# Attention on one core: the value products of two blocks of exponentials run behind each other, every second block

## The chip, the cores and the metric

The kernel runs on 1 core of one Trainium2 chip. The metric is the time of one execution on the device, in microseconds (us); lower is better. TensorE (PE in the rows, with its weight loads as PEld), VectorE (DVE), ScalarE (ACT), GpSimd (POOL) and SyncE (SP) each work through their own list of instructions in order, and wait for one another by semaphores.

## The reference

Two transformer layers of attention and feed-forward over x of 2 x 1024 x 256, in float32. The change touches the two attentions alone. Of these (cut; layer a has one key and value head shared by 16 query heads, layer b has 16 of each and a bias by distance):

```
qkv = x @ w_qkv + b_qkv
scores = jnp.einsum('bnhd,bmd->bhnm', q, k) / jnp.sqrt(jnp.float32(D))
scores = jnp.where(causal, -jnp.inf, scores)
attn = jax.nn.softmax(scores, axis=-1)
out = jnp.einsum('bhnm,bmd->bnhd', attn, v)
...
x = x + attn_a(layernorm(x)); x = x + ffn(layernorm(x))
x = x + attn_b(layernorm(x)); x = x + ffn(layernorm(x))
```

H = D = 16, 1024 positions, two batch rows.

## The kernel before, in words

Each attention (`attention(l)`, l = 0 and 1) is 8 steps: one step is one batch row and a group of 4 heads. A step computes the scores twice.

**Score units** (`query_major`, L1034): queries on the partitions, one PSUM bank of scores each. VectorE takes the row maximum of each (L1716; L1714 where the diagonal tile is masked in the same pass) and counts `su_used`. 38 units and a small transposition of the maxima make a step. They go to three banks in turn (`SU_BANKS`: bank 3, which is half of the tensor `st_ps`, and the two `su_ps`), so unit n waits until VectorE has finished unit n - 3. The maxima of step s+1 are made while step s runs; by L1745, L1721 to L1727 and three small DMAs (L640) they become extra rows of the queries for that step.

**Pieces** (`key_major`, L1075): keys on the partitions, 512 columns for one head each. ScalarE writes their exponentials into `pt` (L1437). Pieces also have three banks in turn, and piece n waits until ScalarE has finished piece n - 3. Four pieces (4 heads) make a **block**; step 0 of a layer has 10 blocks, the others 9, so that an attention has 73 blocks. `pt` is a ring of four blocks, and GpSimd zeroes the part of diagonal tiles behind the diagonal (L798).

**Values** (`values`, L1092): for one block, float32 matmuls with 32 columns of weights each, four side by side, accumulated in `o_ps`. In the trace, a matmul of this kind is two instructions, so that a block with 4 of them shows as x8, and one with two tiles of keys as x16. When the last block of an output half is in, ScalarE copies that half out (`take_output`, L1428); from the copied sums come inverses (SP's L645, VectorE's L1751, SP's L650 and L656), and GpSimd multiplies.

All is in an order written out by hand. In `attention(l)` of TensorE, after each piece come the units that `UNITS_BEHIND` has for it (about one a piece), and behind piece 1 of block i the values of block i - 2 (`PV_LAG = 2`). Twice per attention two blocks' values already run behind each other (at pieces 12 and 40, ahead of a piece), and once at the end.

## Time and profile before

| | |
|---|---|
| median of 3 runs | 1037.01 us (1034.52 to 1038.93) |
| the profiled execution | 1033.92 us, of which the span of its instructions is 1032.2 us |
| granted TensorE clock, mean | 0.984 of full |
| PE / DVE / ACT / POOL busy | 94% / 73% / 56% / 40% of the span |
| attentions | 55.65 to 299.8 us, and 574.14 to 806.8 us in the trace |
| one step (steps 3 to 5 of the first attention) | 27.94 us |

Busy shares are shares of the whole span. A busy PE is one that has a matmul under way; since matmuls overlap at their ends, a 100% share doesn't tell that it could do no more.

### The profile page before, as it was taken

The page shows a single profiled execution, that of the slowest core. Times are in us where ns is not written, and L with a number is a line of the kernel's source. Part 1 is how long each engine was busy: PE and PEld are TensorE (multiplying, and loading weights), DVE is VectorE, ACT ScalarE, POOL GpSimd, SP SyncE. Part 2 cuts the span into 40 slices and gives each one's busy share as a digit, 9 for nine tenths or more (in the row PEclk, how much of TensorE's full clock was granted, in tenths as well). Part 3 has the DMA queues.
Part 4 walks back from the last instruction along what each step waited for, and adds up shares of the span by engine and source line. Part 5 has one row for each costly group of instructions (what it writes and reads, how often), then busy time and mean ns, then how long its engine had stood idle before and what let it go on. Part 6 is the DMA issues. An engine that isn't in the chain of part 4 may idle for free.

```text
span 1032.2 us, 19370 instructions
## 1 busy us (share of the span) xinstructions
PE 969.5 (94%) x6562; PEld 625.6 (61%) x6562; DVE 750.2 (73%) x1820; ACT 573.1 (56%) x1078; POOL 409.4 (40%) x434
## 2 busy tenths in 40 slices
PE   4888999999889999999999899999999899999997
PEld 3433333333348889988886433443334588899887
DVE  6788888888346686447868988888882668754475
ACT  4525767777753335653445657777777533466432
POOL 3420635322534507716653202323225361374570
PEclk9969999999999999999999999999999999999999
DMA  4720222110205315644239524333401251266351
GB/s 142 189 50 10 66 44 45 42 41 13 48 9 172 125 46 156 187 114 129 82 93 217 137 41 71 64 64 77 75 14 44 84 174 51 82 192 158 118 183 48
DMA packets 66754, 95.40 MB, mean 92 GB/s; under 512 B 19669, under 2 KB 50821, under 8 KB 64599
## 3 DMA queue, kind: packets, MB, share of 16 engines
q1 hardware_dynamic: 46645, 52.74, 18.9%
q10 hardware_dynamic: 13100, 22.53, 8.7%
q0 software_dynamic: 6912, 18.88, 7.2%
q8 instruction: 55, 0.90, 0.4%
q14 instruction: 42, 0.34, 0.1%
HBM read 66.79 MB, written 26.67 MB: 91 GB/s over the span
## 4 chain that ended last, share of the span: by engine, by line
PE 72%; DVE 13%; DMA 4%; issue 3%; ACT 3%; POOL 2%; SPq 1%; ACTq 0%; DVEq 0%; POOLq 0%
PE o_ps L1092 13%; PE st_ps L1075 10%; PE su_ps L1034 8%; PE st_ps L284 7%; PE st_ps L285 6%; PE st_ps L286 6%; PE st_ps L1034 4%; PE o_ps L1232 3%; PE su_ps L1138 3%; PE su_ps L1232 3%; DVE mab L1716 2%; PE st_ps L1267 2%; DVE unread L1714 2%; DVE xn L1595 1%; PE su_ps L284 1%
## 5 line engine op out<-in xcount | busy, mean ns | idle before, releaser
L1437 ACT ACTIVATE pt<-st_ps 128x512 f32<-128x512 f32 (+1 forms) x584 | 314.7, 596 | 159.5 <-PE st_ps L1075 150.8
L1075 PE MATMUL st_ps<-qs,ks 99*128 99x512 bf16 (+9 forms) x768 | 212.5, 329 | 5.4 <-DMA qs<-nmx 3.3
L798 POOL TENSOR_SCALAR_AFFINE_SELECT pt<-pt 128x512 f32<-128x512 f32 x120 | 74.4, 637 | 315.3 <-ACT pt L1437 315.3
L1034 PE MATMUL su_ps<-ks,qs 102*128 102x512 bf16 (+7 forms) x538 | 160.0, 330 | 7.5 <-DVE mc L1716 2.8
L1092 PE MATMUL o_ps<-pt,vp 128*32 128x512 f32 (+3 forms) x1536 | 155.5, 502 | 0.0
L1716 DVE TENSOR_REDUCE mab<-su_ps 128x1 f32<-128x512 f32 (+2 forms) x211 | 137.6, 684 | 13.0 <-PE su_ps L1034 12.2
L1034 PEld LDWEIGHTS su_ps<-ks,qs 96*128 96x128 bf16 (+1 forms) x538 | 51.7, 98 | 109.2 <-DVE mab L1716 45.5
L879 POOL DMA_INDIRECT rows_in<-rows,source x80 | 78.6, 983 | 98.0 <-DVE source L1975 73.7
L1075 PEld LDWEIGHTS st_ps<-qs,ks 99*128 99x128 bf16 (+2 forms) x768 | 73.4, 99 | 65.3 <-ACT pt L1437 16.9
L1714 DVE CUSTOM_DVE_ANT_0 unread<-su_ps,cst 128x384 f32<-128x384 f32 (+1 forms) x168 | 99.4, 612 | 17.8 <-PE su_ps L1034 17.7
L1463 ACT CAST hh<-hf 128x512 fp32r<-128x512 f32 x64 | 39.7, 621 | 123.9 <-DVE hf L1930 121.7
L284 PE MATMUL st_ps<-xt_h,wu 128*128 128x512 f32 x256 | 100.9, 394 | 1.4 <-DVE source_f L1972 0.9
L285 PE MATMUL st_ps<-xt_h,wu 128*128 128x512 f32 x256 | 100.3, 392 | 0.0
L286 PE MATMUL st_ps<-xt_l,wu 128*128 128x512 f32 x256 | 99.7, 390 | 0.0
L889 POOL DMA_INDIRECT back<-outs,pos x64 | 67.6, 1056 | 61.8 <-DMA outs<-rows_out 41.6
L1034 PE MATMUL st_ps<-ks,qs 96*128 96x512 bf16 (+6 forms) x230 | 79.1, 357 | 5.5 <-DVE mc L1716 2.8
L1934 DVE TENSOR_TENSOR hl<-hf,hh 128x512 fp32r<-128x512 f32 x64 | 44.4, 694 | 42.6 <-ACT hh L1463 42.6
L1092 PEld LDWEIGHTS o_ps<-pt,vp 128*32 128x32 f32 x1536 | 35.7, 109 | 63.2 <-issue 38.9
L1716 DVE TENSOR_REDUCE mab<-st_ps 128x1 f32<-128x512 f32 (+2 forms) x99 | 67.7, 684 | 4.8 <-PE st_ps L1034 4.7
L1930 DVE TENSOR_TENSOR hf<-st_ps,sg 128x512 f32<-128x512 f32 x64 | 43.9, 686 | 28.1 <-PE st_ps L286 22.7
L1456 ACT ACTIVATE sg<-st_ps 128x512 f32<-128x512 f32 x64 | 38.2, 597 | 42.1 <-PE st_ps L286 41.9
L2035 DVE TENSOR_TENSOR rx_l<-st_ps,rx_h 128x512 fp32r<-128x512 f32 x40 | 27.6, 691 | 45.2 <-ACT rx_h L1487 45.2
(234 smaller groups left out, 2061.3 us busy)
## 6 DMA issues: line engine op xcount, KB each, us to landing
wu_raw<-w_units_dram SPq DMA_DIRECT2D x32, 384.0 KB, 3.2
outs<-rows_out ACTq DMA_DIRECT2D x40, 256.0 KB, 3.2
q_parts<-hml SPq DMA_DIRECT2D x16, 384.0 KB, 3.3
wexp_raw<-w_units_dram SPq DMA_DIRECT2D x16, 384.0 KB, 6.7
inv<-inverses SPq DMA_DIRECT2D x128, 32.0 KB, 1.8
rows<-xn SPq DMA_DIRECT2D x8, 512.0 KB, 6.0
qs<-q_parts ACTq DMA_DIRECT2D x10, 384.0 KB
k_parts<-hml SPq DMA_DIRECT2D x8, 384.0 KB, 2.9
```

Of the source, the lines that this page charges most:

```text
L284: pe.matmul(out, lh, rh, start=n == 0, stop=False)
L285: pe.matmul(out, ll, rh, start=False, stop=False)
L286: last = pe.matmul(out, lh, rl, start=False, stop=n == len(terms) - 1)
L798: pool.affine_select(block, block, [[0, 4], [1, P]], ALU.is_ge, 0.0, base=0, channel_multiplier=-1).then_inc(masked, 1)
L879: pool.indirect_dma_start(rows_in[:, n % RPAIRS, a, :], None, rows, bass.IndirectOffsetOnAxis(ap=source[:, 2 * i + a:2 * i + a + 1], axis= ...
L889: pool.indirect_dma_start(back[:, n % GBUFS, :], None, outs, bass.IndirectOffsetOnAxis(ap=pos[:, j, t:t + 1], axis=0)).then_inc(back_in[n ...
L1034: last = pe.matmul(out_b[:, c0:c0 + width], query_columns(s, slice(0, rows), j0 + a, P * qt, P * qt + P), key_stack(l, s)(j0 + a)[0:rows, ...
L1075: last = pe.matmul(out_b[:, at:at + hi - lo], key_stack(l, s)(j)[0:rows, P * kt:P * kt + P], query_columns(s, slice(0, rows), j, lo, hi), ...
L1092: last = pe.matmul(o_ps[32 * j:32 * j + 32, lo:hi], vp[:, QT * b + kt, 4 * g + j if l else 4 * (g % 2), :], exponentials(S, q)[:, j, at:at ...
L1437: act.activation(exponentials(S, q)[:, j, 0:width_of(s, q)], bank[KM_BANKS[i % len(KM_BANKS)]][:, 0:width_of(s, q)], ACT.Exp, scale=1 / np ...
L1714: dve.tensor_tensor_reduce(unread[ADDED.index(u) % 2][:, 0:width], src, later_keys[:, CH - width:CH], 1.0, LEAST, ALU.add, ALU.max, to).th ...
L1716: dve.tensor_reduce(to, src.rearrange("p (j k) -> p j k", j=share), AX.X, ALU.max).then_inc(su_used, 1)
```

## The change

Values no longer run one block at a time. `RUNS` says behind which block's piece 1 which blocks' values run, `EARLY_RUNS` ahead of which block's first piece, `LAST_RUN` what is left for the end. From block 10 on, the values of blocks i and i+1 run behind piece 1 of block i+3. The older of the two then waits a block longer, so that all four places of the ring are in use. In step 0 the runs are blocks 3 and 4, 5 and 6, and then 7, 8 and 9 ahead of step 1. The end has three blocks in place of two. An attention has 36 runs in place of 70 (each over the same 73 blocks). `take_output` moves with the run that completes the half, and the first reciprocal of a step moves from ahead of unit 6 to ahead of unit 9.

```
+def value_runs():
+    first = len(FIRST_BLOCKS)
+    runs = {2: (0,), 6: (3, 4), 8: (5, 6)}
+    early = {HALF_BLOCKS: (1, 2), first: (7, 8, 9)}
+    for i in range(first, block_base(STEPS) - PV_LAG - 1, 2):
+        runs[i + 1 + PV_LAG] = (i, i + 1)
+    done = max(b for run in runs.values() for b in run) + 1
+    return runs, early, range(done, block_base(STEPS))
...
+def taking(b):
+    i = run_behind(b)
+    if i is None:
+        i = next((i for i, run in EARLY_RUNS.items() if b in run), None)
+    return None if i is None else 4 * i + 3
...
-INVERT_AT, DIVIDE_BEHIND = (6, 27), (2, 4)
+INVERT_AT, DIVIDE_BEHIND = (9, 27), (2, 4)
...
-                    if n in (HALF_PIECES, FIRST_PIECES):
-                        for early in range(i - PV_LAG, i):
-                            values(l, 0, early)
+                    if j == 0:
+                        for b in EARLY_RUNS.get(i, ()):
+                            values(l, *place_of_block(b))
                     key_major(l, s, q, j)
-                    if j == PV_BEHIND and i >= PV_LAG and i not in [*range(HALF_BLOCKS, HALF_BLOCKS + PV_LAG),
-                                                                    *range(len(FIRST_BLOCKS), len(FIRST_BLOCKS) + PV_LAG)]:
-                        values(l, *place_of_block(i - PV_LAG))
+                    if j == PV_BEHIND:
+                        for b in RUNS.get(i, ()):
+                            values(l, *place_of_block(b))
...
-                for q in range(len(LATER_BLOCKS) - PV_LAG, len(LATER_BLOCKS)):
-                    values(l, STEPS - 1, q)
+                for b in LAST_RUN:
+                    values(l, *place_of_block(b))
...
-                        if s and n == 4 * PV_LAG - 1:
+                        own = piece_base(s) + n
+                        if s and own == taking(block_base(s - 1) + last_of(s - 1, 1)[0]):
                             take_output(S - 1, 1)
-                        if n == 4 * (last_of(s, 0)[0] + PV_LAG + 1) - 1:
+                        if own == taking(block_base(s) + last_of(s, 0)[0]):
                             take_output(S, 0)
```

On TensorE, blocks 2 and 3 of step 3 of the first attention, before the change. L1034 and L1038 are score units, L1075 pieces, L1092 values. First behind block 2's piece 1, where the values of block 0 stand alone:

```order
L1034 MATMUL su_ps<-ks,qs 128x512
L1075 MATMUL st_ps<-qs,ks 128x384
L1075 MATMUL st_ps<-qs,ks 128x128
L1092 MATMUL o_ps<-pt,vp 32x512 x4
L1034 MATMUL su_ps<-ks,qs 128x512
L1075 MATMUL st_ps<-qs,ks 128x384
```

and then behind block 3's piece 1, where the values of block 1 stand alone:

```order
L1034 MATMUL st_ps<-ks,qs 128x512
L1075 MATMUL st_ps<-qs,ks 128x512
L1092 MATMUL o_ps<-pt,vp 32x512 x4
L1034 MATMUL su_ps<-ks,qs 128x512
L1075 MATMUL st_ps<-qs,ks 128x512
```

In the changed kernel (its line numbers are 30 higher) the same stretch has nothing between unit and piece at the first place, and both blocks at the second:

```order
L1105 MATMUL st_ps<-qs,ks 128x128
L1064 MATMUL su_ps<-ks,qs 128x512
L1105 MATMUL st_ps<-qs,ks 128x384
...
L1064 MATMUL st_ps<-ks,qs 128x512
L1105 MATMUL st_ps<-qs,ks 128x512
L1122 MATMUL o_ps<-pt,vp 32x512 x8
L1064 MATMUL su_ps<-ks,qs 128x512
L1105 MATMUL st_ps<-qs,ks 128x512
```

The values of block 0 moved behind four more pieces and five more units, and stand ahead of those of block 1 with nothing between.

On ScalarE, from the middle of step 3 of the first attention into step 4: L1437 (later L1467) are exponentials, L1415 (L1445) issues of loads, L1428 (L1458) the copies of a finished output half. Before:

```order
L1415 DMA qs<-q_parts 16x4096
L1437 ACTIVATE pt<-st_ps 128x512 x10
L1428 COPY ou<-o_ps 128x512
L1437 ACTIVATE pt<-st_ps 128x512 x10
L1415 DMA qs<-q_parts 48x4096
L1437 ACTIVATE pt<-st_ps 128x512 x6
L1428 COPY ou<-o_ps 128x512
```

and in the changed kernel, from the same load on:

```order
L1445 DMA qs<-q_parts 16x4096
L1467 ACTIVATE pt<-st_ps 128x512 x14
L1458 COPY ou<-o_ps 128x512
L1467 ACTIVATE pt<-st_ps 128x512 x6
L1445 DMA qs<-q_parts 48x4096
L1467 ACTIVATE pt<-st_ps 128x512 x8
L1445 DMA qs<-q_parts 32x4096
L1467 ACTIVATE pt<-st_ps 128x512 x2
L1458 COPY ou<-o_ps 128x512
```

Both copies stand behind four more exponentials: that of step 3's first half (steps 1, 3, 5 and 7 have it so), and that of step 3's second half, which comes in step 4 (and likewise in steps 2 and 6).

## Rows read from the trace of the kernel before

**Rows 1.** Page, busy time of the engines in the whole span.

```profile
span 1032.2 us, 19370 instructions
PE 969.5 (94%) x6562; PEld 625.6 (61%) x6562; DVE 750.2 (73%) x1820; ACT 573.1 (56%) x1078; POOL 409.4 (40%) x434
```

**Rows 2.** Window of step 3: length, busy time (instructions), clock, DMA share, GB/s.

```profile
core 0: us, PE busy (x) PEld busy (x) DVE busy (x) ACT busy (x) POOL busy (x), PEclk, DMA share, GB/s
160.23:188.17 27.94, 27.52 (x210) 10.78 (x209) 24.59 (x62) 20.41 (x39) 10.77 (x11) 1.00 0.20 41
```

**Rows 3.** Timeline, TensorE around one run of values: start, length, engine, instruction.

```profile
170.41 0.38 PE L1075 MATMUL st_ps<-qs,ks 99*128 99x512 bf16 x1
170.72 1.06 PE L1092 MATMUL o_ps<-pt,vp 128*32 128x512 f32 x8
171.72 0.39 PE L1034 MATMUL su_ps<-ks,qs 96*128 96x512 bf16 x1
171.94 0.38 PE L1075 MATMUL st_ps<-qs,ks 99*128 99x512 bf16 x1
```

**Rows 4.** Timeline, TensorE, two blocks behind each other (512 and 256 columns), second attention.

```profile
612.05 1.50 PE L1092 MATMUL o_ps<-pt,vp 128*32 128x256 f32 x16
613.48 0.39 PE L1075 MATMUL st_ps<-qs,ks 105*128 105x512 bf16 x1
```

**Rows 5.** Timeline, VectorE around the run of rows 3; in brackets idle before.

```profile
171.24 0.68 DVE L1716 TENSOR_REDUCE mab<-st_ps 128x1 f32<-128x512 f32 x1
172.14 1.29 DVE L1716 TENSOR_REDUCE mab<-su_ps 128x1 f32<-128x512 f32 x2 [0.23 <-PE su_ps L1034]
```

**Rows 6.** Groups by shape in step 3: VectorE's score maxima, busy and idle before them.

```profile
L1716 DVE TENSOR_REDUCE mab<-su_ps 128x1 f32<-128x512 f32 x10 | 6.6, 686 | 1.3 <-PE su_ps L1034 1.3
L1714 DVE CUSTOM_DVE_ANT_0 unread<-su_ps,cst 128x384 f32<-128x384 f32 x6 | 3.3, 543 | 0.6 <-PE su_ps L1034 0.6
L1714 DVE CUSTOM_DVE_ANT_0 unread<-st_ps,cst 128x512 f32<-128x512 f32 x4 | 2.7, 687 | 0.2 <-PE st_ps L1034 0.2
L1714 DVE CUSTOM_DVE_ANT_0 unread<-su_ps,cst 128x512 f32<-128x512 f32 x4 | 2.7, 688 | 0.4 <-PE su_ps L1034 0.4
L1716 DVE TENSOR_REDUCE mc<-su_ps 128x4 f32<-128x512 f32 x1 | 0.7, 694 | 0.3 <-PE su_ps L1038 0.3
```

**Rows 7.** Waits in step 3, longest: engine, tile and line, what it waited for; us, times, longest.

```profile
PEld su_ps L1034 <- DVE mab L1716: 3.8, 5, 0.8
```

**Rows 8.** Timeline, VectorE around the two blocks of rows 4.

```profile
613.28 0.07 DVE L1714 DVE_READ_ACCUMULATOR2_ANT mc<- 128x1 f32 x1
614.13 0.69 DVE L1714 CUSTOM_DVE_ANT_0 unread<-st_ps,cst 128x512 f32<-128x512 f32 x1 [0.78 <-PE st_ps L1034]
```

**Rows 9.** Timeline, the same place of the first attention, TensorE and then VectorE.

```profile
101.92 2.53 PE L1092 MATMUL o_ps<-pt,vp 128*32 128x256 f32 x16
104.38 0.61 PE L1075 MATMUL st_ps<-qs,ks 99*128 99x512 bf16 x1
...
105.45 0.69 DVE L1714 CUSTOM_DVE_ANT_0 unread<-su_ps,cst 128x512 f32<-128x512 f32 x1 [2.23 <-PE su_ps L1034]
```

**Rows 10.** Windows ahead of and around the run of rows 9, and in step 7.

```profile
96.00:100.00 4.00, 2.18 (x20) 1.21 (x18) 3.48 (x12) 1.04 (x2) 0.00 (x0) 1.00 0.00 0
100.00:104.00 4.00, 3.41 (x20) 0.89 (x20) 3.21 (x12) 0.00 (x0) 0.00 (x0) 0.78 0.53 140
271.90:281.90 10.00, 9.49 (x58) 3.32 (x59) 0.25 (x1) 7.77 (x15) 4.67 (x6) 1.00 0.20 54
```

**Rows 11.** Timeline, ScalarE around the run of rows 3.

```profile
172.36 1.09 ACT L1437 ACTIVATE pt<-st_ps 128x512 f32<-128x512 f32 x2 [0.94 <-PE st_ps L1075]
```

**Rows 12.** Timeline, a finished output half: ScalarE's copy, then VectorE's reciprocal.

```profile
277.22 0.59 ACT L1428 COPY ou<-o_ps 128x512 f32<-128x512 f32 x1
279.74 0.25 DVE L1751 RECIPROCAL sums<-sums 128x16 f32<-128x16 f32 x1 [10.53 <-DMA sums<-ou]
```

**Rows 13.** Timeline, end of the first attention, TensorE.

```profile
297.76 2.09 PE L1092 MATMUL o_ps<-pt,vp 128*32 128x512 f32 x16
```

More of the change, by code:

```diff
@@ L161, in place_of_block, with run_behind @@
     return next((s, i - block_base(s)) for s in reversed(range(STEPS)) if i >= block_base(s))
+def value_runs():
[6 more added lines that the diff above has]
+    return runs, early, range(done, block_base(STEPS))
+PV_LAG = 2
+RUNS, EARLY_RUNS, LAST_RUN = value_runs()
+def run_behind(b):
+    return next((i for i, run in RUNS.items() if b in run), None)
+def taking(b):
[3 more added lines that the diff above has]
+    return None if i is None else 4 * i + 3
 def unit_base(S):
@@ L215 @@
 FC_BEHIND = {10 + 3 * t: t for t in range(QT)}
-PV_LAG = 2
 PV_BEHIND = 1
-INVERT_AT, DIVIDE_BEHIND = (6, 27), (2, 4)
+INVERT_AT, DIVIDE_BEHIND = (9, 27), (2, 4)
 QKV = [[("kv", 0), ("q", 0), ("q", 1)],
```

## The prediction

> **What bounds the kernel now.** I read the page first: TensorE is busy 94% of the span and VectorE 73% [rows 1], which invites the view that all that counts is TensorE's time. The shares mix attentions with feed-forward, so next came windows of one step: of 27.94 us TensorE is busy 27.52, VectorE 24.59, ScalarE 20.41 [rows 2]. A busy TensorE isn't yet one that can do no more, since a stalled matmul's neighbours overlap it. So third the waits inside that step: its weight loads for score units wait for VectorE, 3.8 us in 5 waits in the largest group alone [rows 7]. And VectorE waits too: the idle before its score maxima sums to 1.3 + 0.6 + 0.2 + 0.4 + 0.3 = 2.8 us, always for a score unit from TensorE [rows 6]. Fourth the timeline, to see when. It is always the same: while TensorE runs values, it issues no score units. VectorE works through what lies in the three banks and then stands. In the run at 170.72, VectorE is busy until 171.24 + 0.68 = 171.92, which is 1.20 after the run's start, and goes on at 172.14, which is 0.42 after the unit behind the run started at 171.72 [rows 3, 5]. So two engines run in lockstep with little slack either way: TensorE is ahead for a while and waits for a bank, then it is away for values and VectorE waits. Work on VectorE plus its idle time is the step's time, and that sum is what I forecast with.
>
> **What a merged run saves on TensorE.** A run of one block (512 columns) takes from 170.72 to the next unit at 171.72, 1.00 us. One of 512 and 256 columns takes from 612.05 to 613.48, 1.43 us [rows 3, 4]. 256 columns more cost 0.43, so 512 cost 0.86, and 0.14 is paid once per run. Before the run there are 0.31 from the piece's start to the run's, where 0.22 pass between a unit and a piece of the same width (171.72 to 171.94): 0.09 more, also once per run. A merge saves 0.14 + 0.09 = 0.23 us, and two blocks of 512 take 1.86. Each attention goes from 70 runs to 36: 34 merges, 68 in all, 68 x 0.23 = 15.6 us, if TensorE's time were all. The end of the first attention shows a dearer pair: 2.03 us, by the record of 2.09 less the 0.06 by which the record of rows 3 (1.06) is longer than that run [rows 3, 13]; there the second block waits for its last exponentials, so I take 1.86 and keep 2.0 as the bound at which nothing is saved.
>
> The Trainium skill (TensorEngine Tiling (Array Packing), Key Properties) says that a change of tiling mode drains the engine. The fixed 0.23 agrees in kind. By that rule alone the sum would be the 15.6 us gain; it stands as the first rival below.
>
> **What it costs VectorE.** How long the banks last after a run's start: mean idle at the nine runs of the step is 2.8 / 9 = 0.31, so VectorE has work for 1.00 + 0.42 - 0.31 = 1.11 us. With a run of 1.86, it stands 1.86 + 0.42 - 1.11 = 1.17 us. There are three banks as before: that cover can't double because the run does. 9 blocks are 4.5 runs a step: 4.5 x 1.17 = 5.3 against 2.8, so 2.5 more. Two things are to be taken off. The idle shown is smaller than the time lost: two maxima behind each other last 1.29 where one lasts 0.68 [rows 5], they overlap by 0.08, which each restart loses; 4.5 restarts fewer give back 0.36. And in every second step the run behind block 7 is gone, where VectorE makes the small parts of the maxima (0.3 idle at `mc` [rows 6]): 0.2 a step. Left: +1.9 us a step.
>
> Bounds: the longest cover I find is 1.30 (613.28 + 0.07 against the start at 612.05 [rows 4, 8]). With 1.25 everywhere, since TensorE has eight pieces in which to fill all banks, it is 4.5 x 1.03 = 4.6, and +1.3 a step; without the 0.2, and with runs of 1.9, +2.3. Does TensorE get that far ahead? Between two merged runs are 8 pieces and about 8.4 units at 0.22 each, 3.6 us; VectorE needs for 8.4 units of 0.60 about 5.0. Yes: it fills the banks, waits for VectorE, and the 0.23 that it saved becomes more waiting for banks.
>
> The mechanism isn't only arithmetic, the trace has it. At the 1.43 us run VectorE stands 0.78 [rows 8]; my formula gives 1.43 + 0.22 (a piece comes before the unit) + 0.42 - 1.30 = 0.77. At the same place in the first attention the run takes from 101.92 to 104.38, 2.46 us (the clock is at half there, 0.78 in the window), and VectorE stands 2.23 us [rows 9, 10].
>
> VectorE makes maxima in steps 1 to 6 but for the last two blocks of step 6, so 12 steps less 2 x 0.2, 11.6 for both attentions: 11.6 x 1.9 = 22 us.
>
> The Trainium skill (Perfetto Trace Analysis, Optimization Strategy) says that the same gap repeating can mean too little PSUM for the next tile. Rows 5 agree, and it speaks against this change, which leaves the three banks and lengthens the gap.
>
> **The rest of the edits.** Step 0: two merges in each attention, 0.4 each in the first and about nothing in the second, +1 (0 to 1.5, my choice by the gaps above). Ahead of step 1 stand three blocks, 0.85 longer than now, less one run's idle of about 0.4: +0.45, and +1 in the first attention where the clock is at half: +1.5. Step 7 has no score units: ScalarE and TensorE share it, ScalarE busy 7.77 and TensorE 9.49 of 10.0 us [rows 10]. ScalarE starves longer per merged run (it stands 0.94 at a run of 1.00 already in step 3 [rows 11]), TensorE saves 0.23 per merge where projections load it: nothing, -1.5 to +2. The end: now the last two blocks take 2.03; with a third ahead of them that once ran 1.5 us earlier, the pieces are issued earlier by as much; nothing, up to +0.5. The ring adds no wait: the place of block i+4 is freed by a run that TensorE issues before that block's first piece. The later copies: from copy to reciprocal pass 279.74 - 277.22 = 2.5 us [rows 12]; now 6 pieces lie between, 4.7 us at 27.94 / 36 a piece, and the reciprocal moved from unit 6 to 9 for it. Hidden by maxima; without that cover it would stop VectorE up to 2.5 us once a step.
>
> Sum: 22 + 1 + 1.5 = 24.5 us. The profiled execution has 1033.9, so 1058.4; it is 3.1 below the median of 1037.0, against which I forecast **1061 us**.
>
> **Rivals.**
> 1. TensorE's time decides, the saving arrives: 1037 - 15.6 = 1021. For it: 27.52 of 27.94 busy, and no TensorE wait of note outside weight loads. Against: VectorE's idle and work alone fill the step, and a longer absence must lengthen the idle unless cover grows to 1.86 + 0.42 - 2 x 0.31 = 1.66, more than any in the trace. From there on the gain begins. 0.11. Another 0.02 for a part of it (covers of 1.5).
> 2. A wash, within 0.5%: cover of about 1.4 to 1.5, so that idle per pair grows by less than 0.3. For it: in parts of the step TensorE isn't yet full ahead, and with eight pieces between runs it always is. 1032 to 1042. 0.08.
> 3. The forecast, VectorE starved at each run, 1051 to 1070. 0.74.
> 4. Beyond it something more: ScalarE starves as well and its lateness meets VectorE's in TensorE's order, or the clock falls to half as behind the stretch with TensorE 2.18 of 4.0 us busy [rows 10]. After the change a step has TensorE at some 25.5 of 29.8, far from that. Above 1070. 0.05.
>
> **How the numbers follow.** A measurement here tells about 0.5% from no change. Faster is 0.13, same 0.08, slower 0.79. The likeliest case's own range comes from the bounds: 11.6 x 1.3 - 0.5 = +14.5 gives 1051, 11.6 x 2.3 + 6 = +33 gives 1070. This holds 0.74; to leave out no more than 0.2 the range goes down over the wash: 1037 to 1070.
>
> **What would show it.** In the changed trace: runs of two blocks 1.86 us from start to the next unit; steps 1 to 6 of 29 to 30.5 us instead of 27.94, those with an even number, which have five runs, longer than those with four; VectorE's idle before score maxima 5 us a step in gaps of 1.0 to 1.3, all released by TensorE; more weight-load waits for VectorE; no reciprocal waiting for its sums. If instead the gaps are 0.6 or less, my cover is wrong, and the kernel is faster. If steps are longer but the gaps aren't at the runs, the cause is another.

## The result and the profile after

The changed kernel takes 1093.71 us (median of 4 runs, 1093.08 to 1095.71) against 1036.09 for the kernel before on the same chip: ratio 1.0555, 95% interval 1.0537 to 1.0572. That is 57.6 us slower. The direction was forecast, the size wasn't (1061 us), and the time lies outside the range.

From the page after, the line that answers to [rows 1], and two groups before which the idle time (behind the last bar) grew, from 5.4 and 17.8 us:

```profile
PE 998.1 (91%) x6562; PEld 632.6 (58%) x6562; DVE 750.8 (69%) x1820; ACT 570.2 (52%) x1078; POOL 409.6 (38%) x434
...
L1105 PE MATMUL st_ps<-qs,ks 99*128 99x512 bf16 (+9 forms) x768 | 217.3, 333 | 21.6 <-DMA qs<-nmx 13.9
...
L1745 DVE CUSTOM_DVE_ANT_0 unread<-su_ps,cst 128x384 f32<-128x384 f32 (+1 forms) x168 | 98.9, 610 | 45.9 <-PE su_ps L1064 45.8
```

No engine is busier in its share: TensorE's fell from 94% to 91%, VectorE's from 73% to 69%. The second row holds what no step of the forecast had: TensorE waits 13.9 us for transfers of the maxima (3.3 us before).

Windows after, of steps 2 and 3 of the first attention, the last 3.7 us of step 3, and the first 4 us of step 4 (columns as in [rows 2]):

```profile
137.55:170.01 32.46, 31.50 (x225) 11.68 (x226) 23.24 (x58) 19.66 (x37) 12.07 (x14) 0.93 0.15 35
170.01:203.53 33.52, 28.86 (x194) 10.81 (x193) 25.87 (x65) 20.86 (x40) 10.27 (x11) 0.95 0.17 34
...
199.80:203.53 3.73, 1.34 (x5) 0.32 (x6) 2.48 (x10) 1.90 (x4) 0.00 (x0) 1.00 0.05 9
203.53:207.53 4.00, 4.00 (x27) 1.26 (x27) 0.86 (x3) 1.20 (x2) 0.00 (x0) 0.57 0.41 91
```

A step takes 32.5 and 33.5 us where [rows 2] had 27.94; 29.8 was forecast. At the end of step 3 TensorE is busy for 1.34 of 3.73 us, and right behind it the granted clock is 0.57, mostly the lower level of 1.2 GHz. From the start of step 0 to that of step 7 the attentions take 27.2 and 28.5 us longer, 55.7 of the 59.6 us between the two spans (1032.2 and 1091.8); the rest lies between and behind the attentions.

A merged run after, TensorE and then VectorE (timeline; answers to [rows 3, 5]):

```profile
212.51 1.92 PE L1122 MATMUL o_ps<-pt,vp 128*32 128x512 f32 x16
214.36 0.39 PE L1064 MATMUL su_ps<-ks,qs 96*128 96x512 bf16 x1
...
213.03 0.68 DVE L1747 TENSOR_REDUCE mab<-su_ps 128x1 f32<-128x512 f32 x1
214.79 0.69 DVE L1747 TENSOR_REDUCE mab<-su_ps 128x1 f32<-128x512 f32 x1 [1.09 <-PE su_ps L1064]
```

The run takes 1.85 us to the next unit, and VectorE stands 1.09 us where it stood 0.23 [rows 5] (0.08 more in each, if the overlap of two maxima is counted as the forecast did: its 1.17). At this run the forecast's size is in the trace to the digit; over whole steps it is checked in e1 below, where the queue doesn't disturb it.

The end of step 3 after, in order of time: VectorE's last part of the maxima, ScalarE's copy of the finished first half, SyncE's two issues, TensorE's first piece of step 4:

```profile
195.14 0.28 DVE L1758 TENSOR_TENSOR nmx<-nmr,nmx 32x128 bf16<-32x128 f32 x1
...
199.15 0.58 ACT L1458 COPY ou<-o_ps 128x512 f32<-128x512 f32 x1
...
199.75 0.58 SPq L675 DMA_DIRECT2D sums<-ou  x1
200.38 1.82 SPq L670 DMA_DIRECT2D qs<-nmx  x3
...
203.53 0.56 PE L1105 MATMUL st_ps<-qs,ks 99*128 99x512 bf16 x1 [2.37 <-DMA qs<-nmx]
```

The maxima are ready at 195.42, but their transfers leave at 200.38. SyncE issues in order, and ahead of them stands the transfer of the first half's sums, which waits for the copy. The same place before:

```profile
182.46 0.59 ACT L1428 COPY ou<-o_ps 128x512 f32<-128x512 f32 x1
...
183.43 0.60 DVE L1727 TENSOR_TENSOR nmx<-nmr,nmx 32x128 bf16<-32x128 f32 x1
...
183.08 0.59 SPq L645 DMA_DIRECT2D sums<-ou  x1
184.06 1.83 SPq L640 DMA_DIRECT2D qs<-nmx  x3
```

There the copy came first, and the maxima left 0.03 us after their last part. Now the copy, which moved with its run, is the later of the two in odd steps.

### The profile page after: what moved, and what is told of

Its sections match the earlier page's. It is cut to its first block, busy times and chain, and to the rows that moved or that the text cites. A ratio compares the mean times of both kernels' runs of the same rounds, so it can differ in the third digit from the quotient of the medians.

```text
span 1091.8 us, 19370 instructions
## 1 busy us (share of the span) xinstructions
PE 998.1 (91%) x6562; PEld 632.6 (58%) x6562; DVE 750.8 (69%) x1820; ACT 570.2 (52%) x1078; POOL 409.6 (38%) x434
## 3 DMA queue, kind: packets, MB, share of 16 engines
q1 hardware_dynamic: 46645, 52.74, 17.8%
## 4 chain that ended last, share of the span: by engine, by line
PE 62%; DVE 17%; issue 7%; DMA 6%; ACT 3%; POOL 3%; SPq 2%; ACTq 0%; DVEq 0%; POOLq 0%
PE o_ps L1122 13%; PE st_ps L1105 6%; PE st_ps L314 6%; PE st_ps L315 6%; PE st_ps L316 6%; PE su_ps L1064 5%; DVE mab L1747 5%; PE o_ps L1262 3%; PE su_ps L1262 3%; PE su_ps L1168 3%; DVE unread L1745 3%; PE st_ps L1064 2%; POOL rows_in L909 2%; DMA qs<-nmx 2%; PE st_ps L1297 1%
## 5 line engine op out<-in xcount | busy, mean ns | idle before, releaser
L1467 ACT ACTIVATE pt<-st_ps 128x512 f32<-128x512 f32 (+1 forms) x584 | 311.4, 602 | 219.3 <-PE st_ps L1105 210.0
L1105 PE MATMUL st_ps<-qs,ks 99*128 99x512 bf16 (+9 forms) x768 | 217.3, 333 | 21.6 <-DMA qs<-nmx 13.9
L1064 PE MATMUL su_ps<-ks,qs 102*128 102x512 bf16 (+7 forms) x538 | 163.5, 335 | 11.4 <-DVE mab L1747 3.9
L1122 PEld LDWEIGHTS o_ps<-pt,vp 128*32 128x32 f32 x1536 | 45.7, 119 | 74.8 <-issue 58.6
L1745 DVE CUSTOM_DVE_ANT_0 unread<-st_ps,cst 128x512 f32<-128x512 f32 (+1 forms) x88 | 54.9, 624 | 16.8 <-PE st_ps L1064 16.8
```

The source lines that it names most:

```text
L1064: last = pe.matmul(out_b[:, c0:c0 + width], query_columns(s, slice(0, rows), j0 + a, P * qt, P * qt + P), key_stack(l, s)(j0 + a)[0:rows, ...
L1105: last = pe.matmul(out_b[:, at:at + hi - lo], key_stack(l, s)(j)[0:rows, P * kt:P * kt + P], query_columns(s, slice(0, rows), j, lo, hi), ...
L1122: last = pe.matmul(o_ps[32 * j:32 * j + 32, lo:hi], vp[:, QT * b + kt, 4 * g + j if l else 4 * (g % 2), :], exponentials(S, q)[:, j, at:at ...
L1467: act.activation(exponentials(S, q)[:, j, 0:width_of(s, q)], bank[KM_BANKS[i % len(KM_BANKS)]][:, 0:width_of(s, q)], ACT.Exp, scale=1 / np ...
L1745: dve.tensor_tensor_reduce(unread[ADDED.index(u) % 2][:, 0:width], src, later_keys[:, CH - width:CH], 1.0, LEAST, ALU.add, ALU.max, to).th ...
```

## The experiments

Ratios are to the kernel before in the same set of runs, with 95% intervals; it had 1036 to 1038 us in two sets and 1072 to 1075 in four (see the end), so step lengths are compared as well. Steps are read as pairs, odd and even, since merged runs fall four to the one and five to the other.

**The queue apart from the runs.** e1: the changed kernel, SyncE's order turned.

```
+                    if s == 0:
+                        gather_sums(S, 0)
-                    gather_sums(S, 0)
                     if s + 1 < STEPS:
                         send_maxima(l, s + 1)
+                    if s:
+                        gather_sums(S, 0)
```

> The changed kernel with one edit on SyncE: in steps 1 to 7 the three small transfers of the next step's maxima are issued ahead of the transfer of the first half's sums, and no longer behind it. Queue theory (the copy of the first half came four exponentials later in odd steps, SyncE waits for it ahead of the maxima, and so TensorE waits at the start of steps 2, 4 and 6, after which its clock falls): waits for the maxima's transfer at a step's start fall from 13.9 us to under 4, most of the half clock in the attentions goes, time 1058 to 1070. Bank theory alone (VectorE starved 1.17 us at each merged run, and nothing else matters): steps of about 29.8 us would already be all of it, the time stays near 1094. If the banks cost nothing and the queue all: 1021 to 1036.

Measured: 1.0246 (1.0231 to 1.0261), 26.6 us over before. Windows of e1, steps 2 and 3:

```profile
132.87:163.15 30.28, 29.33 (x226) 11.17 (x225) 24.43 (x64) 20.14 (x39) 12.06 (x14) 1.00 0.17 37
163.15:192.51 29.36, 27.07 (x194) 10.57 (x193) 24.64 (x60) 20.15 (x39) 10.25 (x11) 1.00 0.20 39
```

Mean 29.82, which is 1.88 over 27.94. (Over steps 2 to 5 of both attentions the mean is 30.07; one of these eight has a fall of the clock in it.) VectorE's idle before its score maxima is 9.6 us in these two steps, 4.8 a step, in nine gaps of 0.8 to 1.2, one for each merged run: the picture that the forecast named ahead. In steps 2 and 3 of the changed kernel it was 17.4 us, the longest gap 3.8. Less than half of the 57.6 us is left once the queue is turned.

e2: the kernel before with single runs, its copy four pieces later in odd steps, and the first reciprocal of a step three units later.

```
-INVERT_AT, DIVIDE_BEHIND = (6, 27), (2, 4)
+INVERT_AT, DIVIDE_BEHIND = (9, 27), (2, 4)
-                        if n == 4 * (last_of(s, 0)[0] + PV_LAG + 1) - 1:
+                        if n == 4 * (last_of(s, 0)[0] + PV_LAG + 1 + s % 2) - 1:
```

> The kernel before, its values one block at a time, with one piece of the change alone: in odd steps ScalarE's copy of the first half stands four exponentials later, and the first reciprocal ahead of unit 9 in place of 6. Queue theory: SyncE issues the maxima some 2.5 us later in steps 1, 3 and 5 of both attentions, the margin at the step's start was about 0.4, so about 2 us in 6 steps, 12 us, and with falls of the clock up to 22: 1046 to 1060. Bank theory: no change, 1036, idle of VectorE at a run still 0.31.

Measured: 1.0179 (1.0164 to 1.0195), 19.9 us over. No run is merged, and yet the longest group of TensorE's waits is this:

```profile
PE st_ps L1075 <- DMA qs<-nmx: 12.4, 8, 2.9
```

The late copy and the late reciprocal cost by themselves nearly as much as the merged runs. Not all of it is the wait for the maxima: step 1 of the second attention takes 33.42 us, where e1 and e3 have 28.64 and 28.19, and in it VectorE's reciprocal waits for its sums. SyncE and then VectorE there:

```profile
654.32 3.43 SPq L656 DMA_DIRECT2D inv<-inverses  x4
657.79 0.61 SPq L645 DMA_DIRECT2D sums<-ou  x1
...
661.92 0.25 DVE L1751 RECIPROCAL sums<-sums 128x16 f32<-128x16 f32 x1 [3.54 <-DMA sums<-ou]
```

The sums' copy had ended at 651.60; their transfer stood behind the inverses' in the same queue. The kernel before has no such wait at this place. e2 doesn't separate the reciprocal's shift from the copy's.

e3: values three blocks behind, runs single (`runs[i + 1 + PV_LAG] = (i,)` for all blocks), maxima sent first.

> The changed kernel with the maxima's transfers issued first, and with the values one block at a time again from block 10 on, but each three blocks behind (so all four ring places are used, and copies stand late, and nothing is merged). Bank theory: VectorE's idle per run is back at 0.3, steps back at about 28 us, time 1033 to 1041. If instead the older values or the full ring cost something, it stays over 1045.

Measured: 0.9995 (0.9975 to 1.0015), steps of 27.95. The ring, the lag, the late copies and the new order together cost nothing; pairing is what costs in e1.

**What the queue and the runs cost together.** e1 and e2 sum to 46.5 us of 57.6. In the trace after, the granted clock is at half for 3.4 or 6.8 us around the starts of steps 2, 4 and 6, where before it isn't. f1 puts work of TensorE into those waits, and z1 is the changed kernel beside it. (Cut: the wait for the piece's bank moves ahead of the filler, which writes to that bank.)

```
+                if j == 0 and q == 0 and s in (2, 4, 6):
+                    for _ in range(10):
+                        pe.matmul(out_b[:, 0:P], ident, ident, start=True, stop=True)
```

> The changed kernel, and ahead of the wait for the transfer of the maxima at the start of steps 2, 4 and 6 of each attention ten fp32 matmuls of the identity with itself (128 columns each, by the sizes of the others about 0.2 us each, so 2 us) into the bank that the piece overwrites. They stand in a wait of 2.4 to 3.9 us. Question: in the changed kernel TensorE's granted clock is at half for 3.4 or 6.8 us in eight more places than before the change, four of them in attention steps behind a start of a step that waits for the maxima. Theory A (the clock falls because TensorE stood still at those starts): the falls that begin behind the starts of steps 2, 4 and 6 go, those near other places stay, and the time is 5 to 12 us below that of the changed kernel without the filler, in spite of up to 1 us that the filler may add at each of six starts. Theory B (the falls come from the merged runs' bursts or from something else than the stand-still): the falls stay, and the time is 0 to 6 us above.

> The changed kernel itself, on the same chip as the three others of this set, so that they can be compared with it directly: its ratio to the kernel before was 1.056 on another chip. If the chip's own slower feed-forward part (1072 instead of 1036 us for the kernel before) adds the same to both kernels, its ratio here is (1072 + 57.6) / 1072 = 1.054; both theories on the cause (the bank of scores that comes free late plus the queue of transfers that the late copy holds up) expect that.

Measured: z1 1.0549 (1.0521 to 1.0577), f1 1.0399 (1.0375 to 1.0423). Work that computes nothing makes the kernel 13.1 us faster. Timeline of f1 at the start of step 4, then the windows of 4 us on either side:

```profile
198.10 2.40 PE L1102 MATMUL st_ps<-cst 128*128 128x128 f32 x20
200.65 0.39 PE L1108 MATMUL st_ps<-qs,ks 99*128 99x512 bf16 x1 [0.15 <-DMA qs<-nmx]
```

```profile
196.50:200.65 4.15, 3.95 (x28) 2.64 (x26) 2.88 (x11) 2.30 (x5) 0.00 (x0) 1.00 0.05 8
200.65:204.65 4.00, 4.00 (x33) 1.36 (x34) 1.82 (x6) 1.77 (x4) 0.00 (x0) 1.00 0.45 100
```

At this place the clock is 1.00 and not 0.57. The six falls at those starts are gone. At other places (ahead of step 1, inside step 3, in the feed-forward part) they are still there; against z1 one inside step 5 is gone, and two are new, at 290 and 785 us. Those inside odd steps start right behind TensorE's wait for the transposition of the maxima, in the changed kernel as well:

```profile
189.40:193.40 4.00, 2.50 (x15) 0.98 (x13) 3.79 (x11) 3.38 (x7) 0.84 (x2) 1.00 0.08 8
```

The clock falls at 193.4. In the kernel before no fall begins inside steps 1 to 6. An odd step of f1 takes 33.54 or 33.55 us with such a fall, and 31.91 or 32.01 without. Theory A holds, with slightly more than its 12 us. The Trainium skill (TensorE: Matmul & The Clock Gate, What's actually happening) says that a gate sets the clock by how busy TensorE has been of late; these two traces agree. The 13.1 us are of the size of the 11.1 that e1 and e2 leave over; that they are the same microseconds was not measured.

**Why pairing costs 1.9 us a step.** First VectorE is relieved: in h1 (single runs) and h2 (the runs and queue of e1) its maximum of a unit off the diagonal reads 64 of 512 columns, so 7/8 of those columns are left out.

```
+                    if s and not diagonal:
+                        src = src[:, 0:64]
```

> The kernel before, with VectorE's maximum from step 1 on taken over the first 64 of 512 columns of each unit that is not diagonal (16 units a step); the maxima of the other columns are left out, so the exponentials differ in value but not in number. VectorE's busy time in a step falls from 24.6 of 27.9 us by 16 times about 0.45 us = 7 us or more, and units no longer wait for it. Both theories expect TensorE (27.5 us of a step busy by the records) to set the time then: 5 to 20 us faster than before, the time of a step 26.8 to 27.7 us. It is here for the next kernel.

> The changed kernel with the same shortened maxima, and with SyncE sending the maxima ahead of the sums of the first half (as in the run that had the merged runs without the held-up queue). Theory A (the forecast's: a merge itself saves TensorE 0.23 us, and costs only because VectorE has two banks of scores to live on while a run of 1.86 us passes): with VectorE at 17 of 27.9 us it can stand idle in the run and catch up, so merging is a gain here: 8 to 16 us faster than the kernel with short maxima alone (68 merges by 0.23 us = 15.6 us). Theory B (a merged run itself costs TensorE time: by its clock, its reads or the wait for both exponentials): it stays slower than the kernel with short maxima alone by 5 us or more.

Measured: h1 0.9955 (0.9937 to 0.9973), the lower end of what was expected, h2 1.0107 (1.0072 to 1.0141). Windows of step 3 in h1, then of steps 3 and 4 in h2:

```profile
156.18:183.88 27.70, 27.35 (x211) 10.86 (x209) 17.98 (x62) 20.37 (x39) 10.77 (x11) 1.00 0.19 42
```

```profile
159.02:187.35 28.33, 26.43 (x194) 10.68 (x193) 18.14 (x60) 19.73 (x39) 10.27 (x11) 1.00 0.17 41
187.35:215.85 28.50, 27.75 (x226) 11.67 (x225) 18.09 (x64) 19.64 (x39) 10.03 (x12) 1.00 0.18 40
```

With some 6.5 us a step less on VectorE, pairing costs 0.72 us a step (28.42 against 27.70) where it cost 1.88: most of the price hangs on VectorE's work. TensorE is busy 27.09 against 27.35, so it does save something. But my expectation that merging would then gain was wrong, and the whole kernel is 16.6 us slower than h1. Part of it is a wait ahead of the transposition of the maxima, weight loads in an odd step, first h1, then h2:

```profile
PEld su_ps L1059 <- DVE mc L1747: 0.7, 1, 0.7
```

```profile
PEld su_ps L1092 <- DVE mc L1781: 1.7, 1, 1.7
```

A run of values used to stand between the last unit and that transposition, and covered VectorE; every second one is gone. The rest of the 16.6 us isn't in the regular steps: at step 0 of the first attention h2 is 2.1 us longer and at step 1 of the second 5.4, where VectorE's reciprocal waits 3.6 us for its sums and TensorE for VectorE. That isn't the turned order's doing: it is the wait of e2 again, whose order wasn't turned. In h2 the sums leave at 629.47, 8.1 us after their copy, behind the inverses; in h1 they leave 0.03 us after it. At this step of the second attention the wait is 3.0 us or more in six traces (e2, g1, h2, h3, s3, t1), 0.4 to 1.9 in six others, and there is none in the four that have the reciprocal at its old place (the kernel before, e4, h1, m1); f1, s1 and m2 have the reciprocal later and no wait. What decides it is open.

h3 is h2 with the transposition behind the run where it stood in the piece ahead of one; t1 is the same edit on e1, with whole maxima.

```
+    for n in range(FIRST_PIECES, len(behind) - 1):
+        i, j = divmod(n + 1, 4)
+        if j == 1 and i in RUNS and behind[n] and behind[n][-1][1] == len(SU):
+            behind[n + 1].insert(0, behind[n].pop())
```

> The kernel of merged runs with shortened maxima (h2: most columns left out of the maxima), and in the odd steps, where the transposition of the maxima stands in the piece just ahead of a run, it now stands just behind the run. In h2 TensorE stands still 1.53 us ahead of it in an odd step and 0.51 us in an even one; in the kernel with short maxima and single runs 0.51 in both. Theory A (a merge does save TensorE 0.23 us; what took it back in h2 is that a run no longer covers VectorE's last maxima ahead of the transposition): the stall is gone, an odd step takes 27.2 to 27.7 us instead of 28.33, and the kernel is about 6 to 8 us faster than h2, if the clock falls alike. Theory B: the stall moves to the next wait, for a bank of scores, and the steps stay at 28.3 us.

> The changed kernel with the maxima sent ahead of the sums (e1), and the transposition of the maxima behind the run in odd steps, VectorE's maxima whole. In e1 TensorE stands still 1.61 us ahead of the transposition in an odd step. Theory A (VectorE is what fills the step: 24.6 us of work and 4.5 runs by 1.17 us idle make 29.9): moving TensorE's stall saves nothing or 0.5 us a step; ratio 1.020 to 1.025. Theory B (the transposition is a cost of its own beside the banks): 1.0 us off each odd step, 8 us in all, ratio 1.017.

Measured: h3 1.0089 (1.0054 to 1.0125), t1 1.0271 (1.0214 to 1.0329). An odd step goes from 28.33 to 27.87 in h3 and from 29.36 or 29.47 to 29.04 or less in t1, about 0.5 us: most of the stall moved to other waits. For h3 that is between the two theories, for t1 it is A. The ratios don't tell t1 from e1.

**Is it that the blocks touch?** If the run's length of 1.86 us is the trouble, space between its blocks must help. s1 puts one unit between them, s2 two pieces with their units, s3 three.

```
                     if j == PV_BEHIND:
-                        for b in RUNS.get(i, ()):
+                        for b in RUNS.get(i, ())[:None if s == 0 else 1]:
                             values(l, *place_of_block(b))
+                    if j == 3 and s:
+                        for b in RUNS.get(i, ())[1:]:
+                            values(l, *place_of_block(b))
```

(s2; s3 begins at `j == 0`.)

> The changed kernel with SyncE sending the maxima ahead of the sums (as in e1), and from step 1 on the first unit of query-major scores that stood behind a run of two blocks now between its two blocks: the blocks still come in pairs at every second block of exponentials, and the ring is used as in the change, but the bank that comes free in the run is filled after 1.0 us and not after 1.86. Theory A (the cost of the run is that VectorE has 1.11 us of scores for 1.86 us without a new bank): the attention's steps return to 27.9 us, the ratio to 1.000 (0.997 to 1.005), and VectorE's idle times in a run are 0.3 to 0.6 us twice instead of 1.17 once. Theory B (the cost is the pairing itself: a pair of blocks waits for the later exponential, and less of TensorE's work lies in every other block): steps stay at 29.4 to 30.3 us, ratio 1.02.

> The changed kernel with the maxima sent ahead of the sums (as e1), and from step 1 on the second block of a pair two pieces later than the first: two key-major pieces and two or three units of query-major scores lie between them; the pairs still come at every second block of exponentials and use the ring as in the change. Theory A (VectorE runs dry): by the times of s1, where VectorE stood 0.31 us in the first run and 0.93 in the second, the second run now begins about 0.95 us after the first one's end with two more banks filled, so that VectorE stands 0.3 and 0.5 us; a step then has 4.5 pairs by 0.8 us idle instead of 1.24, and takes 28.0 to 28.6 us instead of 29.4 to 30.8; ratio 1.003 to 1.012. Theory B (pairs at every second block cost by themselves, wherever the second block stands): steps stay at 29.4 to 30.8 us, ratio 1.02 to 1.03.

> As s2 (maxima ahead of the sums, pairs at every second block), with the first block of a pair one piece earlier, so that three pieces and their units lie between the two blocks instead of two, and five until the next pair. In s2 the steps stayed at 30.3 and 29.3 us, though theory A's account had wanted 28.0 to 28.6. Theory A as it now stands (TensorE wins 0.16 us a unit on VectorE between runs, and the banks cap what it wins at 1.12 us): every piece of distance gives back 0.2 to 0.7 us a step, the even spacing of four pieces (the kernel before and e3) being 27.94; so here 28.2 to 29.2 us, ratio 1.008 to 1.018. Theory B (pairs at every second block, wherever the second stands): 29.3 to 30.3 us, ratio 1.02 to 1.025.

| pieces between the starts of a pair | kernel | a pair of steps, us | mean | ratio |
|---|---|---|---|---|
| none, blocks touch | e1 | 30.28 + 29.36 | 29.82 | 1.0246 (1.0231 to 1.0261) |
| none, one unit | s1 | 30.81 + 29.86 | 30.34 | 1.0300 (1.0248 to 1.0352) |
| 2 | s2 | 29.31 + 30.30 | 29.81 | 1.0235 (1.0185 to 1.0285) |
| 3 | s3 | 27.95 + 28.96 | 28.46 | 1.0106 (1.0022 to 1.0190) |
| 4, single runs | e3 | 27.95 + 27.95 | 27.95 | 0.9995 (0.9975 to 1.0015) |

s1 and s2 brought nothing back: that the run is one piece of 1.86 us isn't the cause, and theory A as I had it until then fell. The timeline of s2 suggests why, VectorE first:

```profile
172.37 1.28 DVE L1753 TENSOR_REDUCE mab<-su_ps 128x1 f32<-128x512 f32 x2
173.57 0.68 DVE L1753 TENSOR_REDUCE mab<-st_ps 128x1 f32<-128x512 f32 x1
...
176.27 1.29 DVE L1753 TENSOR_REDUCE mab<-su_ps 128x1 f32<-128x512 f32 x2 [0.23 <-PE su_ps L1067]
178.24 0.69 DVE L1753 TENSOR_REDUCE mab<-st_ps 128x1 f32<-128x512 f32 x1 [0.68 <-PE st_ps L1067]
```

```profile
174.84 1.06 PE L1125 MATMUL o_ps<-pt,vp 128*32 128x512 f32 x8
175.84 0.39 PE L1067 MATMUL su_ps<-ks,qs 96*128 96x512 bf16 x1
...
176.29 0.38 PE L1067 MATMUL su_ps<-ks,qs 96*128 96x512 bf16 x1
...
176.82 1.06 PE L1125 MATMUL o_ps<-pt,vp 128*32 128x512 f32 x8
```

VectorE takes a unit in 0.60 us ((173.57 - 172.37) / 2), TensorE makes one with its piece in 0.45 (175.84 to 176.29). Between two runs TensorE wins back 0.15 us a unit and no more. With two units between them, the second run finds VectorE hardly stocked: idle 0.23 at the first and 0.68 at the second, 0.91, against 1.09 for the merged one. On the other side of the pair stand too many units: TensorE could win 0.15 at each, but three banks hold only the forecast's 1.11 us of VectorE's work, and there it waits. By this account the step's excess of TensorE's work must be spread evenly over the units; put in every second block it doesn't pass through the banks. It isn't the whole: VectorE's gaps before score maxima sum to 3.7 us a step in s2 against 4.8 in e1, while its busy time is 25.2 against 24.5, and the step is as long. s3, run after this account was formed, lay in the range that it named (by the ratio and the mean step), and not in its rival's. It also moved the first block of a pair, from behind piece 1 to behind piece 0, which no run took apart from the distance.

g1 gives VectorE a bank directly ahead of the merged run (the edit of e4 below):

> The changed kernel with the maxima sent ahead of the sums (as e1), and where a run of two blocks follows, the units of the piece before stand directly ahead of the run instead of ahead of the key-major piece, so that a bank of scores is filled 0.22 us nearer to the run (the edit of e4 for merged runs). Theory A (VectorE runs dry in the run): its cover of 1.12 us grows by 0.0 to 0.2 us in the 4 or 5 runs of a step, as in e4 (1.30 and 1.37 us in some runs), the steps get 0.3 to 0.8 us shorter than in e1, and the ratio is 1.015 to 1.022 against 1.0246. Theory B (pairing itself): steps and ratio as in e1.

Measured: 1.0209 (1.0155 to 1.0264). Steps 2 and 3 of the second attention take 29.63 + 29.55, 0.3 us a step less than e1's 30.29 + 29.47. But over steps 2 to 5 of both attentions g1 has a mean of 30.08 and e1 of 30.07. Its even steps are each 0.7 us shorter than e1's; in three of its four odd steps the clock falls, in one of e1's. So nothing was gained, and the ratio can't tell it from e1.

**Does a fourth bank take the cost away?** m1 (single runs) and m2 (e1) take a bank from the key-major pieces and give it to the units:

```
-KM_BANKS = (0, 1, 2)
+KM_BANKS = (0, 1)
+def score_bank(n):
+    l, i = divmod(n, unit_base(STEPS))
+    return SU_BANKS[n % 3] if i < unit_base(1) else (*SU_BANKS, 2)[i % 4]
```

> The kernel before (single runs), from the units of step 1 on with four banks for the query-major scores instead of three; the fourth is taken from the key-major pieces, which alternate between two banks instead of three. VectorE then has up to three units of work (about 1.7 us) ahead of it when a run begins instead of two (1.12 us). The run is the base for m2. By theory A (a run is paid where the banks cannot hold VectorE's work for its length) VectorE's 2.8 us of idle time in a step shrinks, but TensorE with 27.5 us busy of 27.94 leaves little to win: 27.4 to 28.0 us a step, unless two key-major banks make TensorE wait for ScalarE's exponentials (0.55 us each), which could add 0.5 to 2 us a step. Theory B (pairing costs by itself) says the same of this one.

> The changed kernel with the maxima sent ahead of the sums (e1) and the same four and two banks as m1. Theory A (between two runs TensorE may only run ahead of VectorE by the banks; with three of them a pair of blocks asks for more than they hold, wherever its second block stands, since TensorE wins only 0.16 us a unit on VectorE, 0.60 us against 0.44): with a fourth bank most of the pairing's cost of 1.9 us a step goes; m2's steps are 0.5 us shorter to 0.7 us longer than m1's. Theory B (pairing costs by itself, by its waits for exponentials or by the uneven TensorE work in itself): m2's steps are 1.5 us or more longer than m1's.

Measured: m1 1.0237 (1.0156 to 1.0318), m2 1.0403 (1.0304 to 1.0502); m2 is 17.7 us over m1. Weight loads' waits in two steps, e1 (132.87 to 192.51) and then m2 (132.72 to 192.84):

```profile
PEld su_ps L1067 <- DVE mab L1750: 7.6, 15, 0.8
...
PEld su_ps L1067 <- DVE mc L1748: 3.0, 6, 0.8
```

```profile
PEld st_ps L1119 <- ACT pt L1481: 16.1, 42, 0.8
...
PEld su_ps L1078 <- DVE mab L1761: 2.5, 3, 0.8
```

The fourth bank does away with most of the waits for VectorE, and two key-major banks put 16.1 us of waits for ScalarE in their place, 8 us a step where m1 has 5.2. Over steps 2 to 5 of both attentions m2 has a mean of 30.6 us and m1 of 29.4. These 1.2 us lie between the two expectations, so neither was met: part of the limit moved to the other set of banks. A fourth bank without that loss wasn't tried; that the cost would go with it stays an inference.

**A better version.** e4: the kernel before, its units moved so that one stands directly ahead of each run as well as behind it.

```
                     key_major(l, s, q, j)
+                    if j == 0 and s and units_only(l, n):
+                        continue
+                    if j == PV_BEHIND and s and units_only(l, n - 1):
+                        for ahead, u in UNITS_BEHIND[l][n - 1]:
+                            query_major(l, ahead, u)
```

> The kernel before with one move on TensorE: in steps 1 to 7 piece 1 comes ahead of the units behind piece 0, so that a run of values has a score unit directly ahead of it and directly behind it. Bank theory: the banks then last 0.2 us longer after a run's start (1.33 in place of 1.11), VectorE's idle per run falls from 0.31 to about 0.1, steps go from 27.94 to 26.8 to 27.5, time 1023 to 1031. If VectorE's idle doesn't set the time (TensorE is full anyway): 1036.

Measured: 0.9968 (0.9948 to 0.9987), 4.0 us, steps of 27.47, at the upper end of what was expected; the time fell less than the 5 us expected at least. The same with three blocks of lag (c1):

> What is left of the change's ring when the runs stay single: values three blocks behind (e3, 0.9995) together with a unit directly ahead of and behind each run (e4, 0.9968). If the two do not touch, the steps take 27.4 to 27.5 us and the ratio is 0.996 to 0.997; if VectorE with 24.6 us is the limit that e4 already reached but for 2.35 us of idle time, lag 3 adds nothing. A rival: the added distance lets a wait for the exponential's fourth piece go, and the ratio is 0.993.

Measured: 0.9974 (0.9948 to 1.0001), steps of 27.47 and no rival's gain. e4 is the fastest that computes everything, by less than half a per cent; c1 can't be told from it.

## Why the prediction was wrong, point by point

- **"A merge saves 0.14 + 0.09 = 0.23 us"**: the first part is right. The merged run takes 1.85 to 1.87 us at the places read with the clock at its upper level, 0.14 less than two of 1.00. The 0.09 ahead of a run I haven't measured apart. With VectorE relieved TensorE is busy only 0.26 us a step less (h2 against h1), where 4.5 merges by 0.23 make 1.0; busy time counts stalled matmuls too, so this doesn't settle the size.
- **"With a run of 1.86, it stands 1.86 + 0.42 - 1.11 = 1.17 us"** and **"+1.9 us a step"**: right in size: 1.09 by the bracket, 4.8 us of idle a step in e1 where 4.5 by 1.17 make 5.3, and 1.88 a step, with 26.6 us over for the whole kernel where the sum said 24.5. Part of that agreement is luck. The reason behind it was too narrow, and the 26.6 hold things that the sum had no term for, such as falls of the clock inside odd steps. I took the length of the run for the cause; s1 and s2 break the run up and pay as much. What seems to count is how TensorE's excess is spread against what three banks carry; s3 bears that out, and m2 couldn't prove it. And 0.5 us of an odd step (h3, t1) is the transposition that lost its cover; the sum had the run that is gone there as a saving of 0.2 a step.
- **"The later copies ... Hidden by maxima"**: this is the step that failed. I priced the later copy at the one reader that I looked at, VectorE's reciprocal. The copy is also what `gather_sums(S, 0)` waits for in SyncE's order, and `send_maxima(s + 1)` stands behind it. A delay of four exponentials used up a slack that was near nothing: before, the maxima left 0.03 us after they were ready, now 5.0 us after, and TensorE's waits for them grow from 3.3 to 13.9 us. Priced at nothing, the late copy (with the late reciprocal) costs 19.9 us alone (e2), and turning the queue takes 31 us off the change (57.6 less 26.6; two sets of runs). Nor was it always hidden at the reader that I did look at: in step 1 of the second attention the reciprocal waits for its sums, 0.4 us in the changed kernel and 3.5 in e2.
- **The rival "the clock falls to half"**, 0.05, set aside with "TensorE at some 25.5 of 29.8, far from that": the mean of a step was the wrong number. What stood ahead of the fall at step 4 were 3.7 us with 1.34 of work, a stand-still that came from the failed step above. f1 shows 13.1 us of it.
- **"The ring adds no wait"**: right (e3, 0.9995). Step 0, **+1 and +1.5**: by the trace after, 1.1 us longer in the first attention and 1.5 in the second, 2.6 against 2.5. **Step 7 nothing**: right, from its first piece to its last are 25.6 us before in both attentions, and 25.9 and 25.6 after. **The end**: from the last piece to the end of the last values are 3.11 us after against 2.40, in both attentions, 0.7 each where I had up to 0.5.
- **"Those with an even number ... longer than those with four"**: right in e1 (30.28 and 29.36). In the changed kernel step 3 of the first attention is longer than step 2 (33.5 and 32.5); in the other pairs the even step is still the longer by 0.5 to 1.0 us, but the queue has a part in both: odd steps end with its wait, and even ones begin with the clock at half. The signs, named ahead, that something else is at work were steps of 31.6 to 33.5 us instead of 29 to 30.5, and gaps of VectorE of up to 3.8 us instead of 1.0 to 1.3.

## What to carry to other kernels

When a producer moves, list every queue that holds a wait for it, and what stands behind that wait in the queue; a consumer that has time to spare says nothing of the one behind it. Two engines that pass work through few banks want it spread evenly: here a saving on one of them that gathered its other work into lumps was paid back at the banks, whether the lumps were whole or two pieces apart. And when you ask whether TensorE's clock will hold, look at the places where the engine stands still, not at the mean of a stage.

## What the runs showed of the hardware that I hadn't expected

- Ten fp32 matmuls that compute nothing (20 in the record, 2.40 us), put in a wait, made the kernel 13.1 us faster: the 4 us behind the wait ran at a granted clock of 1.00 instead of 0.57.
- The same kernel before took medians of 1036.1 and 1037.6 us in two sets and 1071.6 to 1075.5 in four. It was traced in the first set alone, but e3's trace, from one of the four, has steps of the same length (27.95 us) and is 43.3 us longer in all: some 21 of these lie between the attentions and some 21 behind them. The five sets of the experiments ran on five chips; whether the chip is the cause is open.
- A fourth bank for the scores helped neither kernel: m1 lost 2.4% (interval 1.6% to 3.2%) with two key-major banks in place of three, although ScalarE's share of a step was 20.8 of 29.2 us.
